# Preparing the feed-forward stage's first token group inside the last turns of attention

## What is computed

```
h = _layernorm(x, axis=-1) * (1 + cb) + sb
x = x + gb * _L1_ffn_ref(h, ...)

def fwd(x):                                # the feed-forward
    x = fwht(x * SU_ug) / SCALE            # Hadamard transform over 512 channels
    x_up = x @ W_up.T * (Wscale_ug[:INTER] * SCALE)
    x_gate = x @ W_gate.T * (Wscale_ug[INTER:] * SCALE)
    x = jax.nn.silu(x_gate) * x_up
    x = fwht(x * SU_dp) / SCALE            # Hadamard transform over 2048
    return x @ W_down.T * (Wscale_dp * SCALE)
```

## Time and profile before

| | us |
|---|---|
| median of 3 runs | 2205.89 |
| lowest, highest | 2197.26, 2205.98 |
| profiled execution, its own time | 2209.23 |
| its span | 2207.4 |
| TensorE busy | 2005.0 (91%) |
| VectorE, ScalarE, GpSimd busy | 1000.2, 742.6, 732.1 |
| mean granted TensorE clock | 0.955 |

### The profile page before, as it was taken

The page is one execution under the profiler, slowest core; times in us unless marked ns, Lnnn a source line. Parts: engine busy times, 40 slices in busy tenths (PEclk is TensorE's granted clock), DMA queues, the critical chain, the costliest instruction groups (busy, mean ns, idle before and its releaser), DMA issues. The chain is left out here.

```text
span 2207.4 us, 38661 instructions
## 1 busy us (share of the span) xinstructions
PE 2005.0 (91%) x11188; PEld 1316.5 (60%) x11189; DVE 1000.2 (45%) x3238; ACT 742.6 (34%) x1747; POOL 732.1 (33%) x668
## 2 busy tenths in 40 slices
PE   4799869799999999999999389999849999999998
PEld 1666645455555555555555256566528878788787
DVE  2367658334466422222222266676534453443432
ACT  0233327222222222222222067777713333223221
POOL 1144420345555555545554454544121101011000
PEclk8799979999999999999999689999979999999999
DMA  6222523598878888888887211100012121121220
GB/s 233 101 70 71 200 70 101 123 227 201 206 182 194 194 196 210 219 212 196 203 219 176 79 34 32 33 4 4 1 49 67 63 82 58 59 84 62 81 67 19
DMA packets 107128, 258.55 MB, mean 117 GB/s; under 512 B 25488, under 2 KB 29200, under 8 KB 106896
## 3 DMA queue, kind: packets, MB, share of 16 engines
q1 hardware_dynamic: 68240, 163.61, 23.4%
q0 software_dynamic: 35552, 88.63, 19.8%
q10 hardware_dynamic: 3232, 4.95, 0.6%
HBM read 196.55 MB, written 59.54 MB: 116 GB/s over the span
## 5 line engine op out<-in xcount | busy, mean ns | idle before, releaser
L1238 PE MATMUL bank<-arena 128*128 x1272 | 440.3, 489 | 2.1 <-ACT arena L1279 0.9
L1191 POOL DMA_INDIRECT x_sum<-route,arena x158 | 254.4, 1610 | 184.2 <-DVE route L1355 158.9
L1238 PEld LDWEIGHTS bank<-arena 128*128 128x128 f32 x1272 | 229.9, 191 | 134.6 <-issue 8.9
L1255 PE MATMUL bank<-arena 96*128 x632 | 298.9, 595 | 2.1 <-issue 2.0
L1202 POOL DMA_INDIRECT arena<-h_moe,arena x158 | 155.6, 985 | 223.9 <-DVE arena L1349 216.9
L1929 PE MATMUL bank<-x_hi,w_hi 128*128 128x512 f32 x512 | 201.0, 392 | 6.0 <-DVE x_lo L2062 6.0
L1342 DVE SCALAR_TENSOR_TENSOR arena<-arena,bank 128x192 f32<-128x192 f32 x159 | 66.0, 415 | 309.4 <-ACT arena L1274 309.4
L1929 PE MATMUL bank<-x_hi,w_lo 128*128 128x512 f32 x512 | 199.5, 390 | 0.0
L1929 PE MATMUL bank<-x_lo,w_hi 128*128 128x512 f32 x512 | 199.3, 389 | 0.0
L1274 ACT ACTIVATE arena<-bank 128x192 f32<-128x192 f32 x159 | 52.8, 332 | 361.0 <-PE bank L1238 361.0
L1255 PEld LDWEIGHTS bank<-arena 96*128 96x128 f32 x632 | 107.3, 190 | 81.2 <-issue 81.1
(11 more groups left out here) (329 smaller groups left out, 3498.0 us busy)
## 6 DMA issues: line engine op xcount, KB each, us to landing
arena<-in_moe_up SPq DMA_DIRECT2D x64, 768.0 KB, 6.3
ffn_arena<-in_ffn_up SPq DMA_DIRECT2D x64, 512.0 KB, 3.3
arena<-in_moe_down SPq DMA_DIRECT2D x64, 384.0 KB, 7.8
arena<-in_L_wmod SPq DMA_DIRECT2D x12, 1024.0 KB, 6.9
x_sum<-route SPq DMA_DIRECT2D x18, 256.0 KB, 2.8
x_res<-in_L_attn_x SPq DMA_DIRECT2D x1, 4096.0 KB, 18.5
h_moe<-arena SPq DMA_DIRECT2D x16, 256.0 KB, 2.1
x_sum<-x_res SPq DMA_DIRECT2D x16, 256.0 KB, 2.4
```

Source lines behind the costliest of these rows:

```text
L1191: nc.gpsimd.indirect_dma_start(out=x_sum[b], out_offset=bass.IndirectOffsetOnAxis(ap=st_dst[:, b], axis=0), in_=y[:, b], in_offset=None, c ...
L1238: mm = nc.tensor.matmul(psum[2 + b][:, 0:2 * FI], xgT[:, b, k], up_ring[:, bass.ds((e % RING) * UPW + k * 2 * FI, 2 * FI)], start=(k == 0) ...
L1255: mm = nc.tensor.matmul(psum[6 + b][:], hiddenT[:, b, n], down_ring[:, bass.ds((e % RING) * DOWNW + n * C, C)], start=(n == 0), stop=(n == 1))
```

## The change

It takes group 0's preparation up to the block sums out of the feed-forward block and puts it in attention.

- Turns 13 and 14 (`z=(0, 1)` and `z=(2, 3)`): VectorE takes each tile's statistics in front of `sums` and normalises it behind the second `maxima`; GpSimd takes the power behind the q rotation and multiplies and adds behind the key-value rotation. The rows go to the second half of `route`, whose incoming rows have been joined by then.
- Turn 16: TensorE transposes the four tiles into the free score banks before the first `turn_probs`; ScalarE copies one after each `copy_pT`; VectorE does the block sums (`mix`) behind tile 14's residual addition.
- After the last key-value product, SyncE fetches the scale columns and weight slices 0 to 2 (the columns a little earlier), the slices over wq and wkv. The feed-forward's memory is laid out so that these are its first three raw buffers; only slice 3 is fetched behind the barrier.
- Behind the barrier stay the four transforms, each with a bank of its own (`x_bank`), and the splits. Counts in the waits of later groups are shifted by the four tiles.

The diff, cut:

```diff
@@ -1422,6 +1425,13 @@
+    assert EARLY * RAW <= KC * C + KC * 2 * NKV1 * HD
+    hz = route[:, KC * GN:].rearrange("p (i c) -> p i c", i=GT)
+    hzT = route[:, 0:KC * GN].rearrange("p (k n) -> p k n", k=KC)
+    z_st, z_r = cv(GT, 8), cv(GT)
+    assert cv.at <= TAIL, cv.at
+    (z_stats, z_rstd, z_xhat, z_done, zT_mm, zT_out, z_in) = (
+        psem("b_" + n) for n in ("z_stats", "z_rstd", "z_xhat", "z_done", "zT_mm", "zT_out", "z_in"))
...
@@ -1439,8 +1449,9 @@
         tile = lambda t: t if 0 <= t < NT else None
+        first_rows = {NT - 3: (0, 1), NT - 2: (2, 3)}
         for m in range(-3, NT + 2):
-            turn(y=tile(m + 3), p=tile(m + 2), f=tile(m + 1), s=tile(m), a=tile(m - 1), w=tile(m - 2))
+            turn(y=tile(m + 3), p=tile(m + 2), f=tile(m + 1), s=tile(m), a=tile(m - 1), w=tile(m - 2), z=first_rows.get(m, ()))
...
@@ -1479,8 +1490,15 @@
         schedule(turn)
+        sp.dma_start(ffn_scales[:, 0:2], a["ug_cols"]).then_inc(z_in, 16)
+        sp.dma_start(ffn_scales[:, 2], a["su_dp_cols"]).then_inc(z_in, 16)
+        sp.wait_ge(kv_mm, NT)
+        for r in range(EARLY):
+            at = TAIL + r * RAW
+            sp.dma_start(arena[:, at:at + RAW].rearrange("p (k h n) -> p k h n", k=KC, h=2), a["ffn_up"][r]).then_inc(z_in, 16)
             sp.wait_ge(rope_in[b], 16 * NT // 2)
+        sp.wait_ge(z_in, 16 * (2 + EARLY))
...
@@ -1521,6 +1539,9 @@
                 rotate(p, slice(0, NHEAD), 0, NHEAD).then_inc(roped_q, 1)
+            for i in z:
+                pool.wait_ge(z_stats, i + 1)
+                nc.gpsimd.tensor_tensor(z_r[:, i:i + 1], z_st[:, i, 7:8], neg_half[:], ALU.pow).then_inc(z_rstd, 1)
...
@@ -1529,6 +1550,11 @@
                 rotate(p, slice(NHEAD, NQK), 2, NKV1).then_inc(roped, 1)
+            for i in z:
+                pool.wait_ge(z_xhat, i + 1)
+                st.did(mul(hz[:, i], hz[:, i], mod[:, 1, 4]))
+                st.settle()
+                nc.gpsimd.tensor_tensor(hz[:, i], hz[:, i], mod[:, 1, 3], ALU.add).then_inc(z_done, 1)
...
@@ -1571,6 +1597,9 @@
                     copy_pT(a, c)
+                if a == NT - 1:
+                    act.wait_ge(zT_mm, c + 1)
+                    copy(hzT[:, :, c * P:(c + 1) * P], psum[c][:].rearrange("p (k n) -> p k n", k=KC)).then_inc(zT_out, 1)
...
@@ -1638,6 +1667,13 @@
                 nc.tensor.matmul(b_r[:, 0:NKV1 * HD], spread, v[0:META, 0].rearrange("p h d -> p (h d)"), start=True, stop=True).then_inc(meta_mm, 1)
+            if a == NT - 1:
+                pe.wait_ge(mx_done, NHEAD * NT)
+                for i in range(GT):
+                    pe.wait_ge(z_done, i + 1)
+                    for k in range(KC):
+                        mm = nc.tensor.transpose(psum[i][:, k * P:(k + 1) * P], hz[:, i, k * P:(k + 1) * P], ident[:])
+                    mm.then_inc(zT_mm, 1)
...
@@ -1767,7 +1803,37 @@
             nc.vector.tensor_scalar(st1[:, 7:8], st1[:, 7:8], EPS, None, ALU.add).then_inc(stats, 1)
+        def z_statistics(i):
+            dve.wait_ge(x_out, i + 1)
+            absorb()
+            st.did(nc.vector.bn_stats(z_st[:, i, 0:6], x_res[:, i]))
+            absorb()
+            st.did(nc.vector.bn_aggr(z_st[:, i, 6:8], z_st[:, i, 0:6]))
+            st.settle()
+            nc.vector.tensor_scalar(z_st[:, i, 7:8], z_st[:, i, 7:8], EPS, None, ALU.add).then_inc(z_stats, 1)
+        def z_rows(i):
+            dve.wait_ge(z_rstd, i + 1)
+            dve.wait_ge(z_stats, i + 1)
+            dve.wait_ge(x_sums, NT)
+            nc.vector.tensor_scalar(hz[:, i], x_res[:, i], z_st[:, i, 6:7], z_r[:, i:i + 1], ALU.subtract, ALU.mult).then_inc(z_xhat, 1)
+        def mix():
+            dve.wait_ge(zT_out, GT)
+            hzM = hz.rearrange("p i c -> p (i c)").rearrange("p (k n) -> p k n", k=KC)
+            pairs = lambda x, n: x.rearrange("p (x two n) c -> p x two n c", two=2, n=n)
+            sv, dv = pairs(hzT, 1), pairs(hzM, 1)
+            for x in range(KC // 2):
+                st.did(nc.vector.tensor_tensor(dv[:, x, 0], sv[:, x, 0], sv[:, x, 1], ALU.add))
+                st.did(nc.vector.tensor_tensor(dv[:, x, 1], sv[:, x, 0], sv[:, x, 1], ALU.subtract))
+            st.settle()
+            sv, dv = pairs(hzM, 2), pairs(hzT, 2)
+            st.did(nc.vector.tensor_tensor(dv[:, 0, 0], sv[:, 0, 0], sv[:, 0, 1], ALU.add))
+            st.did(nc.vector.tensor_tensor(dv[:, 0, 1], sv[:, 0, 0], sv[:, 0, 1], ALU.subtract))
+            st.settle()
...
@@ -1792,6 +1858,8 @@
                 nc.vector.tensor_tensor(qk[:, p % 2, 0:NHEAD].rearrange("p h d -> p (h d)"), bb[:], bqk_row[:, 0:C], ALU.add).then_inc(q_rows, 1)
+            for i in z:
+                z_statistics(i)
...
@@ -1802,6 +1870,8 @@
                 nc.vector.tensor_scalar(h, x_res[:, y], st1[:, 6:7], r1[:, 1:2], ALU.subtract, ALU.mult).then_inc(xhat, 1)
+            for i in z:
+                z_rows(i)
...
@@ -1815,6 +1885,8 @@
                 nc.vector.tensor_tensor(x_res[:, w], ba[:], x_res[:, w], ALU.add).then_inc(x_out, 1)
+            if a == NT - 1:
+                mix()
...
@@ -1839,27 +1911,32 @@
     w_hi, w_lo = fr("w_hi", 2, KC, 2, P), fr("w_lo", 2, KC, 2, P)
-    x_hi, x_lo = fr("x_hi", KC, GN), fr("x_lo", KC, GN)
     in_hi, in_lo = fr("in_hi", 2, GN), fr("in_lo", 2, GN)
-    arena = ph.enter_context(nc.sbuf_tensor("ffn_arena", [P, RING * KC * 2 * P + GN + 64], F32))
+    x_hi = fr("x_hi", KC, GN)
+    below = FT * C + 2 * RAW * 2 + 2 * GN * 2 + KC * GN
+    ph.enter_context(nc.sbuf_tensor("ffn_gap", [P, TAIL - below], F32))
+    raw_early = [arena[:, at:at + RAW].rearrange("p (k h n) -> p k h n", k=KC, h=2) for at in range(TAIL, TAIL + EARLY * RAW, RAW)]
+    arena = ph.enter_context(nc.sbuf_tensor("ffn_arena", [P, RING * RAW + GN + 64], F32))
+    x_lo = fr("x_lo", KC, GN)
     inner = cv(GN)
-    scales, su_dp = cv(2, FT), cv(FT)
+    scales, su_dp = ffn_scales[:, 0:2], ffn_scales[:, 2]
     gate_bank, up_bank = psum[4], psum[5]
+    x_bank = lambda g, k: psum[k] if first(g) else psum[6 + k % 2]
...
@@ -1881,15 +1958,19 @@
+    def raw_of(g, f):
+
+        return raw_early[f] if first(g) and f < EARLY else raw[:, f % RING]
+
-        eng.wait_ge(w_in[f % RING], g * (16 * FT // RING) + 16 * (f // RING + 1))
+        early = 1 if f % RING < EARLY else 0
+        if not first(g) or f // RING + 1 > early:
+            eng.wait_ge(w_in[f % RING], g * (16 * FT // RING) + 16 * (f // RING + 1 - early))
     def _(sp):
-        sp.dma_start(scales[:], a["ug_cols"]).then_inc(scale_in, 16)
-        sp.dma_start(su_dp, a["su_dp_cols"]).then_inc(scale_in, 16)
-        for r in range(RING):
+        for r in range(EARLY, RING):
...
@@ -1931,21 +2012,19 @@
             b = i % 2
-            wait_tile(pe, h_done, 1, t)
-            wait_tile(pe, hT_out, 1, shift(t, -2))
+            wait_tile(pe, h_done, 1, shift(t, -GT))
+            wait_tile(pe, hT_out, 1, shift(t, -GT - 2))
         def transform(g, k):
-            wait_tile(pe, mixed, 1, g)
-            if k >= 2:
+            wait_tile(pe, mixed, 1, shift(g, -1))
+            if k >= 2 and not first(g):
                 wait_tile(pe, x_lo_done, KC, g, k - 1)
-            nc.tensor.matmul(psum[6 + k % 2][:], had[:], hT[:, k], start=True, stop=True).then_inc(xT_mm, 1)
+            nc.tensor.matmul(x_bank(g, k)[:], had[:], hT[:, k], start=True, stop=True).then_inc(xT_mm, 1)
         def prepare():
-            for i in range(GT):
-                transposes(i, i)
...
@@ -1994,21 +2073,21 @@
         def copy_hT(t, i):
-            wait_tile(act, hT_mm, 1, t)
+            wait_tile(act, hT_mm, 1, shift(t, -GT))
             wait_tile(act, xT_mm, KC, g, k + 1)
-            nc.scalar.copy(x_hi[:, k], psum[6 + k % 2][:]).then_inc(x_hi_done, 1)
+            nc.scalar.copy(x_hi[:, k], x_bank(g, k)[:]).then_inc(x_hi_done, 1)
             wait_tile(act, up_mm, 1, shift(n, -2))
-            nc.scalar.copy(w_hi[:, f % 2], raw[:, f % RING]).then_inc(w_hi_done, 1)
+            nc.scalar.copy(w_hi[:, f % 2], raw_of(g, f)).then_inc(w_hi_done, 1)
...
@@ -2113,16 +2190,11 @@
         def prepare():
-            dve.wait_ge(scale_in, 32)
             rest_w(0, 0)
-            for t in range(GT):
-                stats_of(t)
-                xhat_of(t, t % 2)
-            mix(0)
```

More of the change, by code:

```diff
@@ L51 @@
 DVE_F = 21
-ARENA = 24120
+ARENA = 24128
 UPW, DOWNW = KC * 2 * FI, 2 * C
@@ L58 @@
 SCRATCH0 = KEPT + NT * E + E + 2 * C
-TAIL = 16820
+TAIL = 16824
 TEND = TAIL + NT * E + 2 * E + 2
+RAW = KC * 2 * P
+EARLY = 3
 WMB = 3
@@ L1472, in _, with turn @@
                 tables = a["rope"].rearrange("(t p) k d -> t p k d", p=P)
-                def turn(y, p, f, s, a, w):
+                def turn(y, p, f, s, a, w, z):
                     if y is not None:
@@ L1916, in _ @@
                 norm(1, 1)
-                with pool.Fori(0, NT // 2 - 1) as i:
+                with pool.Fori(0, (NT - GT) // 2 - 1) as i:
                     st.loop(i, 2)
@@ L1920, in _ @@
                     norm(i * 2 + 3, 1)
```

(5 more changed lines are left out.)

20 lines of the change are left out of this document (10 added, 10 removed).

## The result

| us | before | after |
|---|---|---|
| median (4 runs each) | 2205.93 | 2185.72 |
| lowest, highest | 2197.26, 2209.25 | 2180.99, 2188.56 |
| profiled execution, its own time | 2209.23 | 2188.56 |
| its span | 2207.4 | 2186.8 |
| TensorE busy in it | 2005.0 | 2005.2 |

The changed kernel is faster: ratio 0.9905, 95% interval 0.9885 to 0.9924, 20.2 us from median to median. 26.05 us were forecast.

A forecast was written before the change was run, and what follows sets the result against it. TensorE was taken as the bound, idling longest at the hand-over from attention to feed-forward. -32.45 there and +6.40 in attention give -26.05 us: 2209.23 becomes 2183.2, or 2180 as a median; range 2171 to 2189.

The forecast's parts named there:

- a low clock at the hand-over: Rival: half clock in the transforms behind the barrier, +3.7 us, 2183.5 us; chance 0.11, shared with late weights.
- The hand-over's 32.45: Attention to feed-forward: barrier to the stage's first product shrinks from 37.60 to 5.15 us, a gain of 32.45 us.
- eight instructions: Behind the barrier: four transforms are eight TensorE instructions of 128x512 in fp32, together 3.70 us.
- last split to first product: Behind the barrier: from the start of the last split to the stage's first product, 1.36 us.
- barrier to product: Hand-over: transforms 3.70, semaphores 0.09 and last split 1.36 make 5.15 us from barrier to the stage's first product.
- Turn 13: Attention: two tiles' statistics on VectorE ahead of the sums, with no slack, put 2.20 us on the path.
- Turn 14: Attention: two tiles' statistics again cost all of 2.20 us, as TensorE already idles 1.06 us for the maxima.
- Normalising at 0: Turns 13 and 14: two VectorE normalising instructions a turn are covered by TensorE's work and cost 0; upper bound 0.8 us.
- Turn 16: Attention: 16 transposes cost 0.95 us, ScalarE's fourth copy 0.50, the block sums ahead of tile 15's division 0.55.
- The fetch: Behind the barrier: fetching four slices took about 4 us before; slice 3, needed three slices later, is hidden.
- Four persistent columns more and new addresses: no cost. Later groups of the stage keep their instructions: 0: Feed-forward stage behind its first product: moved buffers and unchanged instructions add 0 us.
- attention pays more: Rival: VectorE and GpSimd waits in turns 13 and 14 add to the path, 2184 to 2190 us; chance 0.13.

The follow-up runs named there:

- e7: The changed kernel with all four raw weight slices fetched behind the barrier again, as before the change: 2196.63 us in a single run.
- e4: The changed kernel with three unread products put into TensorE's wait ahead of its second scores in turn 14: 2185.57 us in a single run.
- e1: The changed kernel with the scratch ahead of x_lo made 8 floats longer, so that x_lo starts 32 bytes further on: 2172.08 us in a single run.
- e11: The changed kernel with the scratch ahead of x_lo 4 floats longer, meant as 16 bytes but rounded up to 32: 2179.44 us.

## Why the prediction was right, and where not

**The size: inside the range, outside the narrow forecast.** The gain was placed rightly and 20.2 us large for 26.05. The time of 2185.72 lies in the stated range (2171 to 2189), but not in the band of 2177 to 2183 that had been given 0.60. The upper part of the range was there for dearer attention and a low clock at the hand-over; what filled most of it was the stage's loss of 6.3 us, which neither the sum nor a rival had named. That the range held is therefore partly luck, and the 2.05 us of scatter ahead of all pieces worked in the prediction's favour too.

**Sign and place of the gain: right.** The hand-over's 32.45 was measured at 32.47. Its terms held one by one: eight instructions 3.69 (3.70), last split to first product 1.36 (1.36), barrier to product 5.12 (5.15). That the fetch was worth being early is shown by e7.

**The clock at the hand-over: right in this kernel, and with less margin than it looked.** It stayed at 1.00 after a wait of 2.04 us. e4 has the same wait and 0.50, alone among eight traces with this hand-over; it cost 1.7 us in a rival that had been priced at 3.7. The Trainium skill (TensorE: Matmul & The Clock Gate, "Part 4: PE-mode transpose") says that transposes do not count as activity for the full clock. The changed kernel does its 16 from 1600.13 to 1602.10 us and has 1.00 from 1600 to 1603 and at the hand-over, so the trace does not agree. e4 has the same transposes, so they don't tell the two apart either.

**Turn 13: right.** 2.15 for 2.20. **Turn 14: the term was mis-sized.** 2.20 had been taken for it as for turn 13, because the wait grows by as much. It does (2.13), but a wait of 1.06 becomes one of 3.19, the clock halves behind it, and 1.7 us more follow: 3.81. The clock was weighed as a rival at the hand-over alone; the rows for it stood in the same table, and a lengthened wait in attention was not held against them.

**Normalising at 0: right.** The two instructions took 1.16 us together in turn 13 and 1.00 in turn 14, where two beside GpSimd would take 1.63 each, so none was held up by it. The waits' growth of 2.13 us is all of turn 13's 2.15, and of turn 14's 3.81 once the clock is taken off (e4: 19.14 less 17.01), which leaves nothing for the normalising.

**Turn 16: right within 0.3.** 0.82 + 0.86 = 1.68 for 0.95 + 0.50 + 0.55 = 2.00.

**The fetch: a reading that was off and did no harm.** "About 4 us" had been taken from 1622.74 less 1618.07, which is 4.67; the transfer alone took 3.96 in e7. The sum had nothing for it, and it cost nothing.

**"Four persistent columns more and new addresses: no cost. Later groups of the stage keep their instructions: 0": this step failed.** The instructions are the same and each takes longer; the stage paid 6.29 us, the largest miss of the sum. From "the rows repeat" it was concluded that they repeat at the same length. e1 gives the whole of it back by 32 bytes. So it is "new addresses: no cost" that was wrong. It was none of the rivals: the time of 2185.72 lies where "attention pays more" had put it (2184 to 2190), but attention paid 7.6, less than the 10.3 to 12.8 of that rival, and the rest was the stage.

5.46 us of gain are missing between forecast and spans: 6.29 stage + 1.61 turn 14 - 0.32 turn 16 - 0.05 turn 13 - 0.02 hand-over - 2.05 of scatter ahead of all.

## What to carry to other kernels

When a change moves buffers, compare the mean time of the untouched instructions that read them, by operand, and not only their number and waits: 1 to 8 ns on each of 1536 products took 6.3 us from a change that gained 20.2, and a pad of 32 bytes brought them back. Look at the addresses that the arrays really got before reading such an experiment: a pad can be rounded up, as in e11. Price a wait that grows on TensorE with its length and with the clock behind it, and put new work on a feeding engine where that engine waits rather than where TensorE waits for it. When a part is mended, look again at the clock of every place behind it.
